# One semaphore for a whole step of TensorE in a graph layer's edge loop, with turned one-hots made two steps ahead

## The reference

```python
edge_in = concatenate([h[row], h[col], dist], axis=1)      # 53125 x 129
e = silu(edge_in @ eW1 + eb1)                              # 53125 x 128
e = silu(e @ eW2 + eb2)
agg = segment_sum(e, row, num_segments=3125)
out = silu(concatenate([h, agg], axis=1) @ nW1 + nb1) @ nW2 + nb2
x = layernorm(x + out)                                     # 3125 x 64
```

## Time and profile before

| | |
|---|---|
| median of three runs | 834.19 us |
| the profiled execution's own time | 837.93 us |
| its span, first to last instruction | 836.1 us |
| PE matmuls | 653.7 us busy, 78% |
| PE weight loads | 508.5 us, 61% |
| DVE | 479.1 us, 57% |
| ACT | 310.5 us, 37% |
| POOL | 453.4 us, 54% |
| mean granted PE clock | 0.864 of full |
| the 440 indirect DMAs of POOL | 449.8 us, 1.02 us each |

### The profile page before, as it was taken

One profiled execution on the slowest core, in us unless ns is written; L12 is line 12 of the kernel. 1 busy time (PEld: TensorE's weight loads), 2 busy tenths in 40 slices (PEclk: granted clock), 3 DMA queues, 4 the chain that ended last, 5 costly groups with the idle time before them and its releaser, 6 DMA issues.

```text
span 836.1 us, 15563 instructions
## 1 busy us (share of the span) xinstructions
PE 653.7 (78%) x4815; PEld 508.5 (61%) x4815; DVE 479.1 (57%) x1582; ACT 310.5 (37%) x707; POOL 453.4 (54%) x459
## 2 busy tenths in 40 slices
PE   6874749779779877976697749885988787987696
PEld 3453547657667666755575637664766666766585
DVE  6883578997479546755575645684653232212245
ACT  6422222333343333432333323342334334433365
POOL 1056444646666665755576446745666566666500
PEclk9877858879999787979698959986999799889998
DMA  4111110111111111111111011111111111135201
GB/s 122 47 32 45 29 35 26 40 27 45 45 42 42 42 43 38 42 36 36 35 43 42 27 38 39 46 33 38 45 44 44 40 45 42 45 44 47 44 4 39
DMA packets 17077, 34.15 MB, mean 41 GB/s; under 512 B 8118, under 2 KB 9335, under 8 KB 17000
## 3 DMA queue, kind: packets, MB, share of 16 engines
q0 software_dynamic: 14080, 28.86, 14.6%
q1 hardware_dynamic: 2478, 3.36, 1.5%
q10 hardware_dynamic: 442, 0.93, 0.4%
HBM read 30.67 MB, written 2.40 MB: 40 GB/s over the span
## 4 chain that ended last, share of the span: by engine, by line
PE 44%; another core or an unknown queue 21%; DVE 17%; issue 9%; ACT 6%; DVEq 1%; DMA 1%; ACTq 0%
PE e_ps L631 13%; PE pre_ps L631 12%; PE sort_ps L631 8%; PE seg_ps L631 8%; DVE load_hot L1071 4%; PE turn_ps L735 2%; ACT hotT L507 2%; ACT hot L499 2%; DVE agg L1132 2%; ACT e L519 1%; DVE col_hot L1066 1%; DVE row_hot L1067 1%; DVE place L975 1%; DVE count L936 1%
## 5 line engine op out<-in xcount | busy, mean ns | idle before, releaser
L623 POOL DMA_INDIRECT q_rows<-q_table,q_index x440 | 449.8, 1022 | 338.4 <-issue 109.4
L1132 DVE TENSOR_TENSOR agg<-agg,seg_ps 128x125 f32 x416 | 93.5, 281 | 286.3 <-PE seg_ps L631 153.6
L513 ACT ACTIVATE h<-pre_ps,eb_sb 128x512 f32<-128x512 f32 x110 | 75.6, 687 | 370.8 <-remote 249.4
L631 PE MATMUL pre_ps<-ident_f,q_rows 128*128 128x128 f32 x440 | 133.7, 304 | 68.5 <-issue 57.1
L631 PE MATMUL pre_ps<-hotT,p_table 128*128 128x128 bf16 x1320 | 169.1, 236 | 5.0 <-issue 4.8
L631 PE MATMUL e_ps<-w_sb,h 128*128 128x128 f32 x880 | 144.9, 312 | 5.6 <-issue 5.5
L631 PE MATMUL seg_ps<-hot,e 128*128 128x125 f32 x880 | 134.6, 296 | 16.4 <-issue 9.4
L631 PEld LDWEIGHTS pre_ps<-hotT,p_table 128*128 x1320 | 129.0, 105 | 28.1 <-issue 6.9
L631 PEld LDWEIGHTS e_ps<-w_sb,h 128*128 128x128 f32 x880 | 121.2, 212 | 35.7 <-issue 35.5
L631 PEld LDWEIGHTS seg_ps<-hot,e 128*128 128x128 f32 x880 | 121.7, 211 | 21.1 <-issue 16.3
L631 PEld LDWEIGHTS pre_ps<-ident_f,q_rows 128*128 128x128 f32 x440 | 67.7, 154 | 84.6 <-issue 82.2
(11 more groups left out here) (184 smaller groups left out, 478.4 us busy)
## 6 DMA issues: line engine op xcount, KB each, us to landing
q_rows<-q_table,q_index POOLq DMA_INDIRECT x440
q_table<-q_in_sb SPq DMA_DIRECT2D x1, 784.0 KB
x_sb<-in_x_dram ACTq DMA_DIRECT2D x1, 700.0 KB
q_table<-q_in_sb SPq DMA_DIRECT2D x1, 616.0 KB
out_dram<-x_sb SPq DMA_DIRECT2D x1, 364.0 KB
out_dram<-x_sb SPq DMA_DIRECT2D x1, 224.0 KB
w_in<-in_edge_weight_dram SPq DMA_DIRECT2D x1, 185.9 KB
dst_i<-in_dst_dram SPq DMA_DIRECT2D x1, 185.9 KB
```

The costliest lines, as they stand in the source:

```text
L513: A.activation(h1[:, m % 2, :], pre_ps[m % 2][:], ACT.Silu, bias=eb1_sb[:, 0:1]).then_inc(h1_ready, 1)
L623: P.indirect_dma_start(q_rows[:, g % RING, j, :], None, q_table, bass.IndirectOffsetOnAxis(ap=q_index[:, GT * g + j:GT * g + j + 1], axis= ...
L631: return nc.tensor.matmul(o, lhsT, rhs, start=start, stop=stop, **kw)
L1132: D.tensor_tensor(o, o, seg_ps[:, j * LO:(j + 1) * LO], ALU.add).then_inc(agg_added, 1)
```

## The change

- PE's order in a step is now first layer, second layer, the parts of `TENSOR[m]` (sort and others), turn of m+2, segments. In steps up to 103 only the last of them increments a semaphore, `step_ready`. A sort batch still signals by itself when it stands in steps 0 or 1, or when the next batch but one stands in the same step.
- Whoever waited for `pre_ready`, `e_ready`, `seg_ready` or `hotT_ps_ready` of a step up to 103 now waits for `step_ready`: `first_done`, `second_done`, `seg_done`, `turn_done` say for which value. After step 103 the separate semaphores are used, counted from there.
- One-hots are made three steps ahead (`HOT_RING` 5), the turned copies two ahead (`hotT` has three buffers). The turn of `rest` (carry) moves with them.
- ACT does `silu2(m - 1)` before `turned(m + 2)`, and `place_weights(m + 3)` before `convert(m)`.

```diff
-HOT_RING = 4
+HOT_RING = 5
+TURNED = 3
-CARRY_AT = {s: k for s, parts in TENSOR.items() for name, k, i in parts if name == CARRY}
+CARRY_AT = {s + 1: k for s, parts in TENSOR.items() for name, k, i in parts if name == CARRY}
+SORT_STEP = [-1] * len(batches(0)) + [s for s in sorted(TENSOR) for name, k, i in TENSOR[s] if name == SORT]
+SIGNALLED = [n for n, s in enumerate(SORT_STEP) if s < 2 or SORT_STEP[n + 2:n + 3] == [s]]
...
+        def first_done(m):
+            return (step_ready, m + 1) if m <= TIGHT else (pre_ready, m - TIGHT)
+        def second_done(m):
+            return (step_ready, m + 2) if m < TIGHT else (e_ready, m - TIGHT + 1)
+        def seg_done(m):
+            return (step_ready, m + 3) if m < TIGHT - 1 else (seg_ready, m - TIGHT + 2)
+        def turn_done(g):
+            return (hotT_ps_ready, g + 1) if g < 2 else (step_ready, g - 1) if g - 2 <= TIGHT else (hotT_ps_ready, g - TIGHT)
...
             def turned(g):
-                act.wait_ge(hotT_ps_ready, g + 1)
-                if g >= 2:
-                    act.wait_ge(pre_ready, g - 1)
+                act.wait_ge(*turn_done(g))
+                if g >= TURNED:
+                    act.wait_ge(*first_done(g - TURNED))
...
             def silu1(m):
-                act.wait_ge(pre_ready, m + 1)
+                act.wait_ge(*first_done(m))
                 if m >= 2:
-                    act.wait_ge(e_ready, m - 1)
+                    act.wait_ge(*second_done(m - 2))
...
             for m in range(GROUPS):                      # ACT
                 silu1(m)
-                if m + 1 < GROUPS:
-                    turned(m + 1)
                 if 1 <= m <= TIGHT:
                     silu2(m - 1)
+                if m + 2 < GROUPS:
+                    turned(m + 2)
+                if m + 3 < GROUPS:
+                    place_weights(m + 3)
                 convert(m)
-                if m + 2 < GROUPS:
-                    place_weights(m + 2)
...
                 if g >= RING:                            # POOL
-                    pool.wait_ge(pre_ready, g - RING + 1)
+                    pool.wait_ge(*first_done(g - RING))
...
             for m in range(GROUPS):                      # PE
-                first_layer(m)
-                if m + 1 < GROUPS:
-                    turn(m + 1)
+                first = first_layer(m)
+                if m > TIGHT:
+                    first.then_inc(pre_ready, 1)
                 if 1 <= m <= TIGHT:
                     second_layer(m - 1)
-                if 2 <= m <= TIGHT:
-                    segment(m - 2)
-                if m >= TIGHT:
-                    segment(m - 1)
                 for name, k, i in TENSOR.get(m, ()):
                     if name != CARRY:
                         part(name, k, i)
+                if m + 2 < GROUPS:
+                    last = turn(m + 2)
+                    if m > TIGHT:
+                        last.then_inc(hotT_ps_ready, 1)
+                if 2 <= m <= TIGHT:
+                    last = segment(m - 2)
+                if m <= TIGHT:
+                    last.then_inc(step_ready, 1)
+                if m >= TIGHT:
+                    segment(m - 1).then_inc(seg_ready, 1)
...
                 if n >= 2:                               # DVE, sort
-                    dve.wait_ge(sort_mm, n - 1)
+                    if n - 2 in SIGNALLED:
+                        dve.wait_ge(sort_mm, SIGNALLED.index(n - 2) + 1)
+                    else:
+                        dve.wait_ge(step_ready, SORT_STEP[n - 2] + 1)
...
-                    dve.wait_ge(seg_ready, m + 1)        # DVE, add_segments
+                    dve.wait_ge(*seg_done(m))
...
             for m in range(GROUPS):                      # DVE
-                if m + 2 < GROUPS:
-                    one_hots(m + 2)
+                if m + 3 < GROUPS:
+                    one_hots(m + 3)
                 if 3 <= m <= TIGHT:
                     add_segments(m - 3)
```

More of the change, by code:

```diff
@@ L143 @@
 plan()
-assert all((READ, k, 0) in sum((VECTOR.get(s, []) for s in range(SURE[k - 1] // GT - 2)), []) for k in range(1, CHUNKS))
+assert all((READ, k, 0) in sum((VECTOR.get(s, []) for s in range(SURE[k - 1] // GT - 3)), []) for k in range(1, CHUNKS))
 CODED = {0: (0, COL0[1]), 1: (COL0[1], COL0[2]), 2: (COL0[2], COL0[3]), 3: (COL0[3], COL0[4]), 4: (COL0[4], ECOL)}
 CODED_STEP = {3: 2, 8: 3, 10: 4}
-CARRY_AT = {s: k for s, parts in TENSOR.items() for name, k, i in parts if name == CARRY}
+CARRY_AT = {s + 1: k for s, parts in TENSOR.items() for name, k, i in parts if name == CARRY}
+SORT_STEP = [-1] * len(batches(0)) + [s for s in sorted(TENSOR) for name, k, i in TENSOR[s] if name == SORT]
+SIGNALLED = [n for n, s in enumerate(SORT_STEP) if s < 2 or SORT_STEP[n + 2:n + 3] == [s]]
 BAT0 = [sum(len(batches(j)) for j in range(k)) for k in range(CHUNKS)]
@@ L284, in build @@
         hot32 = sb("hot32", [128, 4, GT, LO])
-        hotT = sb("hotT", [128, 2, GT * 128], BF16)
+        hotT = sb("hotT", [128, TURNED, GT * 128], BF16)
         h1 = sb("h1", [128, 2, GT * 128])
@@ L558, in _ @@
             place_weights(1)
+            turned(1)
+            place_weights(2)
             for m in range(GROUPS):
@@ L641, in sort @@
                               a + b == 0, k == 0 and a + b == LOAD[k] - 1)
-                last.then_inc(sort_mm, 1)
+                if n in SIGNALLED:
+                    last.then_inc(sort_mm, 1)
             def part(name, k, i):
@@ L738, in turn @@
                     last = nc.tensor.transpose(restT_ps, rest[:].rearrange("p v b -> p (v b)"), ident_b[:])
-                last.then_inc(hotT_ps_ready, 1)
+                return last
             p_flat = p_table[:].rearrange("p b s f -> p (b s f)")
@@ L757, in first_layer @@
                         last = mm(o, p_flat[:, bass.ds(windows[j] + s * HID, HID)],
-                                  hotT[:, m % 2, j * 128:(j + 1) * 128], False, s == SPLITS - 1)
-                last.then_inc(pre_ready, 1)
+                                  hotT[:, m % TURNED, j * 128:(j + 1) * 128], False, s == SPLITS - 1)
+                return last
             def second_layer(m):
@@ L768, in second_layer @@
                               False, j == GT - 1)
-                last.then_inc(e_ready, 1)
+                return last
             def segment(m):
@@ L778, in segment @@
                               hot32[:, m % 4, j, :], True, True)
-                last.then_inc(seg_ready, 1)
+                return last
             def x_part(n, stop):
@@ L835, in _ @@
             pe.wait_ge(w2_in, 32)
-            turn(0)
+            turn(0).then_inc(hotT_ps_ready, 1)
+            turn(1).then_inc(hotT_ps_ready, 1)
             for m in range(GROUPS):
-                first_layer(m)
-                if m + 1 < GROUPS:
-                    turn(m + 1)
+                first = first_layer(m)
+                if m > TIGHT:
+                    first.then_inc(pre_ready, 1)
                 if 1 <= m <= TIGHT:
                     second_layer(m - 1)
-                if 2 <= m <= TIGHT:
-                    segment(m - 2)
-                if m >= TIGHT:
-                    segment(m - 1)
                 for name, k, i in TENSOR.get(m, ()):
@@ L1195, in _ @@
             one_hots(1)
+            one_hots(2)
             dve.wait_ge(src_rest_in, 32)
```

20 lines of the change are left out of this document (10 added, 10 removed).

## The result

The changed kernel takes 853.5 us (median of 4 runs, 853.0 to 855.7), the kernel before 834.2 beside it: a ratio of 1.024, 95% interval 1.022 to 1.026. It is 19.3 us slower. A second profile of the kernel before (e9, span 821.8) has 199.9 us in steps 4 to 33 where this one has 208.1, so a stage of before can move by some 8 us from one profile to the next.

What follows compares the result with a forecast made beforehand. Bound by waiting: PE's signals come late while POOL gathers, making 6.15 us steps. Terms +14.2 (steps 4 to 33), -12.0 (34 to 77), -1.8 (78 to 103), -4.2 (before 4) sum to -3.8: 834.2 to 830.4, taken as 831; range 811 to 852.

Steps and rivals of the forecast that it cites:

- the loop's price: DVE's add, one-hots, PE's sort, turn, segments in series: 5.7 us an ordinary sort step; +14.2 us over steps 4 to 33.
- segments 0.9: PE's segment matmuls at the end of the loop: 0.9 us, being 1.05 less what overlaps.
- sort 1.2: PE's sort matmuls in the loop, between DVE's one-hots and the turn: 1.2 us.
- 2.4 after a sort: PE's sort, turn and segments before the signal, added to DVE's work in steps 4 to 13: 2.4 us.
- +5 to +14 for the clock: PE's serial chain at 1.2 GHz in half of the dozen steps 4 to 13; kept in the range, outside the sum.
- The holds: Three-step stalls after chunk reads: one signal shortens each to 25.4 us; steps 34 to 77 change by -12.0 us.
- a lucky catch: Hold after a read: the one signal that gets out carries a whole step, DVE doing slots and sort inside: 23.6 us.
- an unlucky one: Hold after a read: signals held after two groups, 12.7, then 6.15, then 8.35: 27.2 us.
- Rival 1: DVE's add behind the one signal: the loop costs, the holds stay; slower, 848 us; chance 0.32.
- Rival 2: PE's signals: fewer get out sooner, steps fall toward POOL's floor of 5.0 to 5.1 us; 808 us; chance 0.16.
- my 0 for it: PE's signals: three increments fewer in 104 steps save 0 us by the trace, against an estimated 8 by the skill page.
- Rival 3: Early stages: POOL's cycle holds everywhere and the sorts hide; no change, 834 us; chance 0.14.

Runs made afterwards that it cites:

- e1: Changed kernel with PE's sorts and other parts issued behind the step's one signal, each sort batch signalling by itself: 805.2 us, 0.972 of before.
- e18: Changed kernel with segments ahead of the sorts behind their own signal, as e5, with late signals: 824.9 us, 0.985 of before.
- e14: The kernel of e6 again, with punctual signals: 740.0 us, 1.092 of before.
- e7: The kernel of e1 with four more PE signals a step that nobody waits for, with punctual signals: 677.9 us, 1.002 of before.
- e2: Changed kernel's order and rings, but separate signals for first layer, second layer, each sort batch, turn and segments: 864.4 us, 1.044 of before.
- e6: Changed kernel with both layers' shared signal ahead of the sorts; sorts, turn and segments signal separately, segments behind sorts: 739.4 us, 1.091 of before.
- e3: Kernel before with only the deeper rings, nothing reordered and no signal shared: 822.0 us, 0.990 of before.
- e5: Changed kernel with segments ahead of the sorts behind their own signal, with punctual signals: 681.3 us, 1.007 of before.
- e12: Kernel before with one of a group's four gathers issued from the seventh group on: 647.9 us, 0.781 of before.
- e8: The kernel of e1 with the read of chunks 4 to 8 one step after their last sort, not two: 681.7 us, 1.007 of before.
- e13: The kernel of e5 again, with punctual signals: 681.8 us, 1.009 of before.
- e16: The kernel of e1 with four buffers of gathered rows, not six: 688.3 us, 1.016 of before.

## Why the prediction was wrong

The stages, in us, of six profiles (late signals: the first four):

| steps | before | after | e1 | e18 | e14 | e7 |
|---|---|---|---|---|---|---|
| 4 to 13 | 79.2 | 96.8 | 75.5 | 78.9 | 96.5 | 74.7 |
| 14 to 20, no sorts | 40.8 | 43.1 | 42.8 | 44.4 | 31.7 | 29.1 |
| 34 to 42, a sort each but the last | 55.9 | 55.1 | 54.2 | 57.1 | 55.1 | 46.3 |
| 43 to 45, after a read | 30.9 | 29.3 | 24.9 | 25.1 | 20.8 | 15.2 |

*The mechanism held.* Wherever the segments stand behind the sort and its window read (the change three times, e2, e6, e14), steps 4 to 13 take 94.7 to 96.8 us and steps 34 to 42 take 54.5 to 57.4, with late signals and without. Those are the loop's own times, set by VectorE and TensorE in series. Before, late signals made steps 34 to 42 last 55.9 anyway, so there the loop was free, as I had it (forecast 55.35); where signals are punctual the same steps could take 46.3, and it costs 9 us a cycle. This is why the change is 2 to 3% slower in late groups and its near relatives some 9% in punctual ones.

*The step that failed* is, first, the loop's price: "segments 0.9", "sort 1.2", and what PE does before the signal, "2.4 after a sort". I took them from the earlier trace rows, where TensorE was busy, and then kept the clock "in the range". But the loop itself makes TensorE idle ahead of each such chain, 4.11 us in step 33 and 6.70 in step 4, and the chain then runs wholly or in part at the low clock: 4.6 and 5.5 us in place of 2.4. The steps with long VectorE work exceed their terms: 4 by 3.1 us (13.8 against 10.7), 7 by 2.2 (12.1 against 9.9), 10 by 3.2 (11.1 against 7.9) and 33 by 2.3 (10.65 against 8.35). That is 10.8 of the 12.7 us by which steps 4 to 33 exceed their forecast. Part of steps 4 and 10 is the twelve matmuls behind the window read: at the 1.18 us of the earlier trace rows for six, a second batch is 1.2 us in each; I had counted one. The range had +5 to +14 for the clock, but in steps 4 to 13 alone; it comes back in the window step of every chunk. No run held the clock up, so its share is read from these rows and not from an experiment.

The Trainium skill's page "TensorE: Matmul & The Clock Gate", section "What's actually happening", gives the array 1.2 GHz when it has been idle and 2.4 when busy. The trace agrees in these rows: 2.16 us against 1.18 for the same six matmuls, with a granted clock of 0.54 over the chain and of 1.00.

*The holds* are the second step that failed. Forecast 25.4, 25.4 and 25.4; measured 29.3, 29.3 and 23.6, so they shortened by 1.6, 1.5 and 1.8 where I expected 5.5, 5.4 and 0. The sum took the middle between a lucky catch, in which VectorE does slots and sort inside the hold (23.6), and an unlucky one, 12.7 + 6.15 for the first two steps and 8.35 for the window step (27.2). What came is the unlucky one: the first two steps took 18.6 us after each of the first two reads (13.1 after the third), and slots and sort start only behind them. The window step, the third, then has the loop at the low clock, 10.8, 10.7 and 10.6 us against 8.35. So the one signal did shorten the hold, by 5.9 us in its first two steps, and the loop took 4.3 of them back. That e1's holds, 24.9 and 25.0, match the forecast of 25.4 is chance: they are the same 18.6 and a step 45 of 6.3 us without the loop.

Together steps 4 to 33 and 34 to 77 exceed their forecasts by 12.7 and 6.6 us, of the 19.5 between the forecast change of the span, -3.8, and the measured one, +15.7. The other 3.6 us up to the medians' +19.3 come from taking the profile's place above the median to carry over; the changed kernel's profile stood at its median.

The hold also looks other than I pictured it. The changed kernel's timeline in step 44:

```profile
413.55 0.27 PE L651 MATMUL seg_ps<-hot,e 128*128 128x125 f32 x1 [0.91 <-issue]
...
414.98 0.27 PE L651 MATMUL pre_ps<-hotT,p_table 128*128 128x128 bf16 x2 [1.05 <-issue]
...
416.39 0.22 PE L651 MATMUL pre_ps<-hotT,p_table 128*128 128x128 bf16 x1 [1.14 <-issue]
...
422.32 0.90 DVE L1163 TENSOR_TENSOR agg<-agg,seg_ps 128x125 f32 x4 [9.89 <-remote]
```

TensorE itself moves in ones and twos, a microsecond apart and waiting for nothing recorded, beside one gather of POOL per 1.25 us. It isn't the signal alone that is late.

*The rivals.* Rival 1 had the sign and, at 848 us, most of the size, and both its reasons have a part: the holds shortened by 1.5 to 1.8 us only, and the clock loss that it mentioned in passing is the larger part. Rival 2's floor is reached in e7, where POOL gathers without a pause, but before, with all its signals, runs in 676 us in that group too: fewer signals are not what it takes. That sharing a signal gives 1 to 2% where signals are late (e1 against e3, the change against e2) goes against my 0 for it. Whether it is their number or what waits for them isn't settled: e7, with four more signals a step at 1.002 of before, ran where none are late. The Trainium skill's 26.3 ns an increment of concurrently running tiles ("TensorE: Matmul & The Clock Gate", "The cost: per-tile semaphore tail") would be an estimate of 11 us for e7's 4 x 104 signals, if it held for matmuls one after another; e1 itself didn't run in that group, but e7 stands only 1.9 us above before, and below e5, which adds none. No run here shows such a tail. Rival 3 fails: the early stages did not hide the loop.

## What to carry to other kernels

Before two producers' results are put behind one signal, follow the consumer's queue back: if it makes what the producer needs ahead of that signal, an open pipeline becomes a loop, and the loop's time is the sum of both engines. Price TensorE's part of such a loop from rows at the low clock, since the loop itself makes it idle (4.6 us, not 2.4), and look up the granted clock of the very step that you price. With the same signal, the parts moved behind it turned +3.2% into -3.0% in one group. And when a kernel stands in a slow regime that hides work, the same edit may cost less there than elsewhere (40 against 58 us).

## What the runs showed of the hardware

The same program took 831 to 840 us in three groups of runs and 676 in two. In the first kind TensorE's completions reach the other engines up to 3 us late in plain steps and over 10 in long streams of gathers, and TensorE's own matmuls come a microsecond apart. In the kernel before, these segments end at 476.44, and the add that waits for them starts at 492.31:

```profile
475.39 1.05 PE L631 MATMUL seg_ps<-hot,e 128*128 128x125 f32 x8
```

With a quarter of the gathers nearly all of it is gone (e12). In the second kind it never occurs with the full number of gathers (e5 to e8, e13, e14, e16). The runs don't tell what sets the kinds apart, nor whether it belongs to the chip.
